# Where in a step TensorE turns the row reciprocals: behind the first head's transposes instead of the third's

## What is computed

```
scores = (q @ k.T) * scale            # a0: also times a decay table; a1: rotary q and k, causal mask
attn   = softmax(scores, axis=-1)
out    = (attn @ v) @ W_o
# a0: self-attention, 16 heads of 16, 512 keys, k and v from a 64-wide latent
# a1: causal self-attention, 16 heads of 64, 512 keys, latent of 128
# x1: attention of 8 heads of 64 over 512 own keys and 64 context keys
```

## Time and profile before

| | us |
|---|---|
| median of three runs | 4008.63 |
| the profiled execution | 4008.86 |
| its span on the core | 4006.7 |
| PE busy in it | 3339.5 (83%) |
| DVE busy | 2300.4 (57%) |
| ACT busy | 1893.5 (47%) |
| POOL busy | 953.0 (24%) |

### The profile page before, as it was taken

One profiled execution on the slowest core, in us unless ns is written; L12 is line 12 of the kernel. 1 busy time (PEld: TensorE's weight loads), 2 busy tenths in 40 slices (PEclk: granted clock), 3 DMA queues, 4 the chain that ended last, 5 costly groups with the idle time before them and its releaser, 6 DMA issues. The chain is left out here.

```text
span 4006.7 us, 74067 instructions
## 1 busy us (share of the span) xinstructions
PE 3339.5 (83%) x25632; PEld 2464.7 (62%) x25632; DVE 2300.4 (57%) x7397; ACT 1893.5 (47%) x4614; POOL 953.0 (24%) x758
## 2 busy tenths in 40 slices
PE   6888888858689589898888977999999939999970
PEld 3656565547678466665666655777777736767650
DVE  4777777758867356656666553566666642222226
ACT  4787778833342165555555534555555512121210
POOL 0000000024200376776667720001111130000014
PEclk8999999977799799999999988999999969999995
DMA  3111111010200121121212211000000051111113
GB/s 107 49 50 49 55 56 67 30 29 1 97 2 1 62 57 49 51 54 49 53 49 54 54 27 54 13 13 20 23 23 23 24 207 32 32 35 34 34 42 109
DMA packets 111257, 187.56 MB, mean 47 GB/s; under 512 B 23792, under 2 KB 66224, under 8 KB 106032
## 3 DMA queue, kind: packets, MB, share of 16 engines
q1 hardware_dynamic: 100000, 131.44, 11.4%
q0 software_dynamic: 10896, 51.39, 3.4%
HBM read 91.93 MB, written 57.28 MB: 37 GB/s over the span
## 5 line engine op out<-in xcount | busy, mean ns | idle before, releaser
L1064 ACT ACTIVATE a_t<-a_t,a_neg 128x512 f32<-128x512 f32 (+3 forms) x1024 | 642.6, 633 | 9.1 <-DVE a_neg L1282 8.2
L891 PE MATMUL a_T<-ident,a_t 128*128 128x128 f32 x3328 | 509.6, 287 | 125.6 <-ACT a_pT L1055 56.7
L891 PEld LDWEIGHTS a_T<-ident,a_t 128*128 128x128 f32 x3328 | 382.1, 145 | 321.2 <-issue 288.3
L1055 ACT ACTIVATE a_pT<-a_T 128x512 f32<-128x512 f32 (+3 forms) x768 | 370.1, 512 | 270.8 <-PE a_T L891 270.7
L1277 DVE CUSTOM_DVE_ANT_0 a_t<-a_A,a_decay 128x512 f32<-128x512 f32 x512 | 323.0, 687 | 99.7 <-PE a_A L856 99.5
L1277 DVE CUSTOM_DVE_ANT_0 a_t<-a_A,a_table 128x384 f32<-128x384 f32 (+3 forms) x512 | 221.0, 487 | 168.1 <-PE a_A L868 166.8
L1113 POOL TENSOR_TENSOR a_rsin<-a_rawswapped,a_sin 128x512 f32<-128x512 f32 x128 | 168.4, 1316 | 557.8 <-DMA a_rawswapped<-a_raw 535.8
L2324 DVE COPY experts_y<-experts_Y 128x256 f32<-128x256 f32 x72 | 30.6, 425 | 438.2 <-PE experts_Y L2262 438.2
L2274 PE MATMUL experts_H<-ex_w,experts_xgT 128*128 x576 | 261.2, 596 | 0.9 <-ACT experts_xgT L2301 0.6
L2262 PE MATMUL experts_Y<-ex_w,experts_hT 128*128 x1152 | 260.5, 379 | 1.0 <-DVE experts_hT L2333 1.0
L2262 PEld LDWEIGHTS experts_Y<-ex_w,experts_hT 128*128 128x128 f32 x1152 | 218.8, 190 | 61.3 <-issue 35.2
(11 more groups left out here) (329 smaller groups left out, 6885.7 us busy)
## 6 DMA issues: line engine op xcount, KB each, us to landing
moe_sent<-a_zeros POOLq DMA_DIRECT2D x33, 1024.0 KB, 8.2
a_rawswapped<-a_raw SPq DMA_DIRECT2D x512, 64.0 KB, 2.0
a_invrep<-a_inv_dram SPq DMA_DIRECT2D x64, 256.0 KB, 3.9
ex_w<-in_f_w_dram SPq DMA_DIRECT2D x16, 1024.0 KB
experts_xg<-moe_sent SPq DMA_DIRECT2D x72, 128.0 KB, 2.0
moe_results<-experts_y SPq DMA_DIRECT2D x72, 128.0 KB, 1.7
x_invrep<-x_inv_dram SPq DMA_DIRECT2D x32, 256.0 KB, 3.9
x_all<-in_x_dram SPq DMA_DIRECT2D x1, 4096.0 KB, 14.4
```

Source lines behind the costliest of these rows:

```text
L891: mm = pe.transpose(bank[:, kt, :], t_of(u, j, kt * P, (kt + 1) * P), sh.ident[:])
L1055: nc.scalar.activation(to, of, ACT.Copy).then_inc(t_empty, 1)
L1064: nc.scalar.activation(t_of(u_e % U, j, 0, n), t_of(u_e % U, j, 0, n), ACT.Exp, bias=neg[:, slot, j:j + 1], scale=SCALE, accum_out=total[: ...
```

## The change

The position of the work "inv" goes from 2 to 0.

```
         found = [(j, ("y", qt)) for qt, (at, j) in enumerate(Y_AT) if prev and at == s]
         if s % QT == LAG_N and (own or (s == LAG_N and prev)):
-            found.append((2, ("inv", (s // QT - 1) % G)))
+            found.append((0, ("inv", (s // QT - 1) % G)))
```

## The result

The changed kernel took 4022.98 us, the median of 20 runs (4014.62 to 4034.85), the kernel before 4006.87 in 20 runs of its own: a ratio of 1.0041, 95% interval [1.0032, 1.0050]. That is 16.4 us slower, 12.8 to 20.0, where 8 were forecast. The profiled execution took 4015.67 us with a span of 4013.5, only 6.8 above the span before. That the two profiles lie so near has to do with the two executions: untouched code between a0 and a1 happened to take 6 us less here, and this execution is among the fastest of its twenty, while the profiled one before (4008.86) is above the median of its own.

What follows compares the result with a forecast made beforehand. It took a0, a1 and x1 as rings of TensorE, VectorE and ScalarE, where delays to all three are not made up. Losses of 13.1 us less gains of 5.1 made 8.0 slower: 4017 us, range 4003 to 4026.

Steps and rivals of the forecast that it cites:

- Rival 2: TensorE's clock: new waits of TensorE could bring clock falls of about 1.2 us each, 4025 to 4042 us; chance 0.17.
- Rival 4: Losses larger than counted: a0's steps 10 and 14 cost more, a0 loses 17.0 instead of 10.8, 4023 us; chance 0.12.
- a0, step 6: Last seven batches: the turn, until now filling head 3's wait, pushes back heads 1 and 3; 7 x 0.44 = 3.1 us lost.
- a0, step 10: Last seven batches: the turn waits for its bank, so head 1 comes later; 7 x 0.4 = 2.8 us lost.
- a0, step 14: First seven batches: turn and head 1 delay the key projection by two times 0.44; 7 x 0.7 = 4.9 us lost.
- a1, step 10: The turn, now in front of head 1, waits for its bank, delaying the transposes 0.33 us; 7 x 0.33 = 2.3 lost.
- three tails: Ends of a0, a1 and x1: the turn begins 1.5 us earlier; 3 x 1.5 = 4.5 us gained.
- a1, last batch: Step 14: the copy, waiting 0.96 us for the turn, can start earlier; 0.6 us gained.
- x1: Outside its tail: router work bounds step 2, step 6 runs gapless; 16 turns between 7 us loss and small gain, taken as 0.
- PEclk of a stage differing by more than 0.01: Sign in the profile after, for any stage's granted TensorE clock: such a difference would show the prediction wrong.
- Rival 1: Absorbed: delays in a0 and a1 vanish in later slack, only tails and last batch remain, 4003.8 us; chance 0.15.
- Rival 3: The spread comes earlier at 16 landing waits in a1's middle, 1.4 us each, 22 us faster, 3995; chance 0.06.

Runs made afterwards that it cites:

- e1: Kernel before with the turn moved behind head 0 in a0 alone, tail included; a1 and x1 as before: 4023.29 us, ratio 1.0029 [1.0016, 1.0043].
- e5: The changed kernel once more, on the second chip, against the kernel before: 3999.37 us, ratio 1.0038 [1.0024, 1.0051].
- e3: Kernel before with the turn moved behind head 0 only in the three tails: 4001.33 us without two left-out runs, ratio 0.9978 [0.9964, 0.9992].

## Why the prediction was right, and where its sizes were off

The direction, the places and the mechanisms stand; the size did not (8 forecast, 16.4 [12.8, 20.0] measured, inside the range of 4003 to 4026). The time lies beyond the forecast's own range (4010 to 4021) and beyond 4020.7, from where on the prediction calls the kernel slower, to which it gave 0.30; that the wide range holds it is owed to the room left for rivals 2 and 4, not to the sum. What the forecast lacked is the clock in a0 and x1's own loss. By the terms of the sum, in us, the measured ones from the profiles:

| term | forecast | measured |
|---|---|---|
| a0, step 6 | +3.1 | +3.1 |
| a0, step 10 | +2.8 | +2.7 |
| a0, step 14 | +4.9 | +6.1 |
| a1, step 10 | +2.3 | not told from 0 |
| three tails | -4.5 | -3.9 |
| a1, last batch | -0.6 | -0.6 |
| x1 | 0 | +3.7, of which some 1.9 clock (+3.1 in the profile after) |
| clock in a0, steps 0, 4 and 9 | 0 | +5.5, +8.6, +12.4 (after, e1, e5) |
| sum | +8.0 | +11.1 without the last row, +16.6 to +23.5 with it |

That the smallest of these sums is so near the 16.4 of the runs proves little: the profile that it comes from was itself only 6.8 us above the one before. Without the clock in a0 the sum is below the measured interval.

- *Step 6: right.* The turn had filled the wait of head 3, and its 0.44 us fell due in full; half a turn costs 0.22 early and nothing late.
- *Step 10: right.* The wait for the bank was shorter than expected (0.37 instead of about 0.6 idle); steps 10 to 12 together grew by 0.38 with 0.4 forecast (step 10 alone by 0.45, step 11 gave 0.38 back, step 12 took 0.31). The loss is the turn's length and not the wait's: half a turn costs 0.17, and the wait for the bank takes the place of the 0.40 us for which head 2 used to wait.
- *Step 14: right in kind, 0.87 a batch for 0.7.* I let the delay of ScalarE's key copy (0.65) pass straight to the ring. By L1282 the projection comes 0.98 later than before (418.64 against 419.44, and 413.01 against 414.79) and ScalarE's copy 0.77 later; turn (0.44) and head 1 (0.43), the "two times 0.44" of the prediction, come out in full, as half a turn with 0.65 and the turn behind head 1 with 0.47 show.
- *a1, step 10: not confirmed.* The wait in front of the turn is there, but the step's seven periods sum to 55.95 after and 56.65 before; over the six profiles with an unchanged middle of a1 the sum is 54.1 to 57.1 (mean 56.3), over the four with the early turn 56.0 to 57.9 (mean 57.1). The term assumed that every delay of TensorE's transposes reaches the next scores at an unchanged pace; yet this step ran below full clock in both, and its periods scatter by several tenths within one profile. a1's length was 970.5 to 976.9 us in six profiles with its middle unchanged and 969.2 to 974.3 in four with the whole turn early: a term of 2.3 can't be seen in that, and may be nothing.
- *Tails and last batch: right.* The waits for the turn are 1.46, 1.39 and 1.46 us shorter (a0, a1, x1). From the last L1282 to the multiplication the means over the profiles with and without the early turn in the tail differ by 1.43 in a0 (12.80, 14.23), 1.15 in a1 (15.77, 16.92) and 1.28 in x1 (19.25, 20.53): a1's and x1's landings take back a little. In a1's last batch step 15 is 0.6 shorter (5.95 to 5.32).
- *x1: wrong.* I read its step 2 from the third batch on, where the router's work hides most of the turn, and priced the first two batches, which have no router work, by the same row. That accounts for 1.05 of the 3.7; the largest other piece is the clock in one step of the first batch.
- *Rival 2, the clock: in part.* It foresaw a loss of 8 to 25 us through the clock on top of the forecast, and a0's steps 0, 4 and 9 lose 5.5 to 12.4. But I had put it at new waits of TensorE making new falls. Idle time now stands in front of 31 turns that had none (21 counted; step 14 and the first batch were left out), but the long steps are 0, 4 and 9, which hold no turn. A fall cost 1.7 us in step 0 and up to 1.6 and 1.4 in steps 4 and 9, where I had 1.2. The Trainium skill (TensorE: Matmul & The Clock Gate, "Part 1: The HAM clock gate") says that the chip's look at TensorE's activity runs freely, so that the place of a change varies from run to run; e3, with its a0 at 772.4 against 757, agrees. Less so the other six profiles of the old order, on three chips, which lie within 3 us, and the two groups of the table in the section on the clock: that six of six new orders lose there and one of seven old ones speaks for a part that belongs to the order, and how the order does it isn't shown. My test, PEclk of a stage differing by more than 0.01, was too coarse for it: of a0 it was 0.97 before and 0.96 after,

```profile
49.93:823.86 773.93, 669.96 (x7566) 450.52 (x7566) 556.87 (x1731) 607.44 (x1475) 15.26 (x29) 0.96 0.13 47
```

  one hundredth, which over 774 us can already hide a loss of more than 5.
- *Rival 1, absorbed: fell* with the periods of steps 6, 10 and 14. *Rival 3: fell*; the landing waits in a1's middle did not shrink. *Rival 4: its time was near, its terms were not*: step 10 cost 0.38 a batch and not 1.1; the missing time was in x1 and in the clock.

## What to carry to other kernels

A small piece of work that stands where its engine waits anyway is free. Moved "earlier", it costs its whole length at the new place, and the old wait comes back at the old one (step 6). So before moving it, look for the idle time that it fills now. Moving it pays where something waits for its result and its engine has little else to do, as in the tails.

Where a piece of work takes a place in a rotation of buffers, look at what now stands behind its wait. The wait for the bank itself cost nothing here: in step 10 it replaced another wait, and in step 14 the projection could not start before the same reading either. What cost in step 14, beside the turn, was head 1, which used to run during that wait and now stood behind it, and this part did not shrink with the moved work.

Price every variant of a step (first, second, later batches), since a stage may have several bounds.

## What was not expected of the hardware

Two kernels with the same order of work in a0 outside its tail (before and e3) had on the same chip an a0 of 757 us in one profile and of 772 in the other, through steps at a lower granted clock, such as 0.81 instead of 1.00 (8.98 instead of 7.29 us). Two profiles can't tell a change of 10 us in such a kernel; the shortest and the median period of each step can, to some hundredths of a us, and 20 runs of each could, to 4 us.

Between the first and the second chip the kernel before differed by 26 us in time. The profiles show where 20 us of it lie: from TensorE's last instruction to the end, which is the combining part, far from the change, it is 121 us in all six profiles of the first chip (121.0 to 122.1) and 101 in all seven of the other two. The ratios of the changed kernel agreed all the same (1.0041 and 1.0038).
